# Self-attention of a fused decoder layer: key tile 1 gets its penalties by a multiplication on GpSimd, not by their logs on TensorE

## What is computed

```python
penalties = res * scope                            # (b, 512, 512), from a gate per position
log_pen = jnp.log(jnp.maximum(penalties, 1e-32))
scores = jnp.einsum('bhqd,bhkd->bhqk', q, k) / np.sqrt(16)
scores = scores + log_pen[:, None, :, :]           # the same for all 16 heads
probs = jax.nn.softmax(scores, axis=-1)
ctx = jnp.einsum('bhqk,bhkd->bhqd', probs, v)
```

## Time and profile before

| | us |
|---|---|
| median of 3 runs | 879.59 |
| lowest and highest | 878.59, 881.4 |
| the profiled execution, its own time | 875.29 |
| its span, first to last instruction | 873.5 |

### The profile page before, as it was taken

How to read it: one execution, slowest core, us unless ns; L and a number is a source line. 1 busy time by engine, 2 the same in 40 slices (tenths; PEclk the granted TensorE clock), 3 DMA queues, 4 the chain that set the end, 5 groups by cost and what they waited for, 6 DMA issues and landing times.

```text
span 873.5 us, 12882 instructions
## 1 busy us (share of the span) xinstructions
PE 707.1 (81%) x4374; PEld 279.8 (32%) x4374; DVE 618.0 (71%) x1576; ACT 482.7 (55%) x800; POOL 328.1 (38%) x417
## 2 busy tenths in 40 slices
PE   6077779998788799998898899996798699965653
PEld 3042223343222243443232433532223134332221
DVE  3978674675698756668967556589876577627996
ACT  3213465555354858744458578444467576954634
POOL 6104656645466404445663034555414011000314
PEclk9588899999999989999999899998989899996965
DMA  3532142120322213211222132223112320000002
GB/s 102 147 113 92 40 94 75 57 64 20 91 60 63 86 31 111 78 40 51 65 67 84 29 89 78 60 75 102 39 39 59 88 63 16 6 1 1 1 1 96
DMA packets 34896, 54.00 MB, mean 62 GB/s; under 512 B 4368, under 2 KB 25872, under 8 KB 34832
## 3 DMA queue, kind: packets, MB, share of 16 engines
q1 hardware_dynamic: 32912, 51.61, 20.7%
q10 hardware_dynamic: 1920, 1.57, 1.1%
HBM read 36.91 MB, written 14.68 MB: 59 GB/s over the span
## 4 chain that ended last, share of the span: by engine, by line
PE 44%; DVE 26%; POOL 11%; ACT 9%; issue 7%; DMA 2%; SPq 1%; ACTq 0%; POOLq 0%; DVEq 0%
PE ps L1447 10%; PE ps L1402 9%; DVE unused L931 7%; PE ps L1422 6%; POOL probs L652 6%; PE ps L1389 6%; PE ps L1305 5%; ACT probs L836 3%; PE ps L1382 2%; POOL rest L678 2%; DMA KS<-parts_kc 2%; PE ps L1426 2%; PE ps L1427 1%; DVE pen_a L994 1%; DVE h_all L1218 1%
## 5 line engine op out<-in xcount | busy, mean ns | idle before, releaser
L1402 PE MATMUL ps<-KS,QS 96*128 96x512 bf16 x512 | 202.8, 397 | 79.4 <-DVE mx L931 52.6
L836 ACT ACTIVATE probs<-ps 128x512 f32<-128x512 f32 x256 | 148.8, 596 | 151.5 <-PE ps L1427 96.7
L652 POOL TENSOR_TENSOR probs<-probs,penT 128x512 f32<-128x512 f32 x128 | 166.9, 1322 | 167.9 <-ACT probs L836 167.5
L931 DVE CUSTOM_DVE_ANT_0 unused<-ps,lp 128x512 bf16<-128x512 f32 x256 | 171.1, 686 | 81.9 <-PE ps L1402 77.8
L1422 PE MATMUL ps<-QS,KS 108*128 108x512 bf16 x512 | 198.2, 390 | 11.5 <-ACT probs L836 11.3
L836 ACT ACTIVATE probs<-ps,mask_col 128x512 f32<-128x512 f32 x256 | 166.4, 688 | 59.0 <-PE ps L1422 57.4
L931 DVE CUSTOM_DVE_ANT_0 unused<-ps,mask_rest 128x512 bf16<-128x512 f32 x192 | 128.2, 685 | 48.7 <-PE ps L1402 47.8
L1402 PEld LDWEIGHTS ps<-KS,QS 96*128 96x128 bf16 x512 | 50.5, 99 | 225.5 <-DVE mx L931 125.7
L1447 PE MATMUL ps<-probs,v_s 128*32 128x256 f32 x1024 | 83.8, 400 | 9.6 <-POOL probs L652 8.8
L1447 PE MATMUL ps<-probs,v_c 128*32 128x256 f32 x1024 | 82.5, 395 | 0.6 <-ACT probs L836 0.6
L678 POOL TENSOR_TENSOR rest<-proj,parts 128x512 f32<-128x512 f32 x32 | 38.3, 1197 | 79.4 <-ACT parts L749 78.8
(11 more groups left out here) (186 smaller groups left out, 969.9 us busy)
## 6 DMA issues: line engine op xcount, KB each, us to landing
parts_qs<-parts SPq DMA_DIRECT2D x8, 384.0 KB, 2.6
parts_ks<-parts SPq DMA_DIRECT2D x8, 384.0 KB, 2.8
QS<-parts_qs SPq DMA_DIRECT2D x16, 192.0 KB
KS<-parts_ks SPq DMA_DIRECT2D x16, 192.0 KB
parts_kc<-parts SPq DMA_DIRECT2D x8, 384.0 KB, 2.5
parts_qc<-parts SPq DMA_DIRECT2D x8, 384.0 KB, 2.8
QS<-parts_qc SPq DMA_DIRECT2D x16, 192.0 KB
KS<-parts_kc SPq DMA_DIRECT2D x16, 192.0 KB
```

Of the source, the lines that this page charges most:

```text
L652: g.tensor_tensor(probs[:, T % NP, :], probs[:, T % NP, :], penT[:, MUL_KT.index(kt), :], ALU.mult)\
L836: s_.activation(probs[:, T % NP, :], ps[:, EXP_BANKS[T % 3], :], ACT.Exp, bias=bias)\
L931: v.tensor_tensor_reduce(out=unused[:, i % 2, :], in0=ps[:, MAX_BANKS[i % 2], :], in1=lp[:, t, :] if kind == "s" else mask_row(b), scale=1 ...
L1402: mm(ps[:, MAX_BANKS[i % 2], :], QS[0:SK, slot, j, t * P:(t + 1) * P], KS[0:SK, slot, j, :], start=True, stop=True).then_inc(max_scores, 1)
```

## The change

One constant. `MUL_KT` lists the key tiles whose penalties are multiplied in on GpSimd; `exp_tile`, `context`, `multiply`, `lpB` and the sizes of `penT`, `lpT_hi` and `lpT_lo` all go by it.

```diff
-MUL_KT = (0, 2)
+MUL_KT = (0, 1, 2)
```

## The result

The changed kernel took **897.19 us** (median of five runs, 895.97 to 905.91) beside 879.70 us for the kernel before in the same sitting: 1.0223 times as long, interval 1.0169 to 1.0277. The prediction said 892.9 us, in a range of 881 to 908, and slower. Sign and size are right. Of the three terms that make up the sum, the first came out within its bounds and the third in its total. The second, the largest, was mis-sized by a factor of two: the slower VectorE operations that it counts came, but it left out GpSimd's queue in those groups and the time at TensorE's half clock.

The account below looks back on a forecast made before the run. TensorE was fullest (81% busy), but self groups were taken as paced by PE, DVE or POOL's queue. Terms -1.8 + 7 + 5.6 + 2.5 = +13.3 us on 879.6 gave 892.9 us, range 881 to 908.

Parts of the forecast that it names:

- first term: Seven self groups (s(b,g): batch b, head group g) that PE paces: POOL's queue eats part of TensorE's saving, -1.8 us.
- walk of s(2,1): POOL's queue followed forward in batch 2, head group 1: key tile 2's context product slightly earlier, net -0.7 us, not -1.73.
- second term: Seven self groups that DVE paces: PE's saving becomes waiting, DVE operations slow beside POOL; +7 us, bounds 0 and +14.
- third term: Groups where a projection's split shares POOL's queue: s(1,1) +5.6 us, bounds +3 and +7; s(2,3) +2.5, bounds 0 and +4.
- its own walk to 224.0: POOL's queue followed in s(1,1): the projection's second low part ends at 224.0 instead of 218.44, +5.6 us.
- GpSimd keeps up: Rival: POOL has room, so nine self groups gain 1.73 us each; 864 us, faster. Chance 0.09.
- The waits are absorbed: Rival: new waits for POOL shorten later row-maximum waits and contention is hidden; 881 us, no change. Chance 0.14.
- The waits let the clock fall: Rival: new PE waits bring four to six falls of TensorE's clock, 10 us more; 903 us. Chance 0.17.
- 64 instructions on each line: Sign: the logs' matmul lines L1426 and L1427 stand 64 times each, where they had 128.
- waits for POOL near 20 us: Sign: context products (L1447) waiting for POOL rise from 8.8 us to some 20 to 30 us.
- L990's median above 0.9 us: Sign: the DVE penalty operation on L990, 0.884 us in the median, rises above 0.9 us.
- the longer wait in s(1,1): Sign: PE waits for `KS<-parts_kc` in s(1,1) longer than 3.5 us.

Follow-up runs that it names:

- second profile: Another profiled execution of the changed kernel, unedited, taken with the experiments: 896.73 us, span 894.8 us.
- the order mended: Changed kernel, but in s(1,1) the four added multiplications stand behind the second low part of the projection's split: 892.48 us, ratio 1.0146.
- the repeat: The changed kernel, unedited, timed again in another sitting beside the kernel before: 900.49 us, ratio 1.0220.
- the opposite move: Against the kernel before, only key tile 0 is multiplied on GpSimd; tiles 1, 2 and 3 get their logs on TensorE: 871.56 us, ratio 0.9903.

## Why the prediction was right, point by point

**The first term was right within its bounds.** The walk of s(2,1) had the context product of key tile 2 at 407.8 instead of 408.55, 0.75 us earlier. In the second profile, in which s(2,1) ran at the full clock, PE has it here:

```profile
419.00 0.64 PE L1447 MATMUL ps<-probs,v_s 128*32 128x256 f32 x8 [1.92 <-POOL probs L652]
```

That group began at 398.83, so it is 20.17 us into the group, 20.93 before: 0.76 us. Behind it stand, on POOL, two rstd instructions and the last pair of multiplications, in the order of the walk:

```profile
415.00 0.23 POOL L634 TENSOR_SCALAR rstd<-mv 128x4 f32<-128x4 f32 x1
415.31 1.04 POOL L635 TENSOR_TENSOR rstd<-rstd,minus_half 128x4 f32<-128x4 f32 x1
416.31 2.53 POOL L652 TENSOR_TENSOR probs<-probs,penT 128x512 f32<-128x512 f32 x2
```

The sum of the seven groups was -0.2 and +1.0 us and not -1.8. The half clock came into some of them: s(3,0) took 21.1 us at the full clock in one profile, and 22.7 us with 3.4 us of half clock in the other, the same instructions. That is not so everywhere: s(0,3) took 21.55 us with 3.4 us of it and 21.43 us with none.

**The second term failed in size, by what it left out.** It held TensorE's saving in these seven groups at zero and charged +7 us for slower VectorE operations. The penalty operations slowed down as priced. But the groups lost 15.1 and 13.8 us, and the five of them that hold penalty operations lose as much without these. Two things were left out. POOL, whose twelve multiplications and five short instructions I walked in the groups that PE paces only, can set the pace in these as well (ten in a row at 1.41 us against a slot of 1.33 us in s(2,2)); PE's waits for POOL in the seven groups rose from 2.8 us to 9.5 and 6.8. And half-clock time in them rose from 23.6 us to 63.7 and 58.4. No run tells how the missing 7 or 8 us divide between the two. Windows of s(2,2) in after and in the second profile:

```profile
429.10:452.00 22.90, 18.99 (x113) 5.29 (x112) 21.52 (x48) 10.60 (x18) 18.30 (x17) 0.83 0.22 57
```
```profile
421.40:445.60 24.20, 19.98 (x113) 5.37 (x112) 23.36 (x51) 10.51 (x18) 18.51 (x17) 0.79 0.22 58
```

In the earlier trace rows it has nine PE records more and 17.91 us of PE at clock 1.00; now fewer matmuls, 19 to 20 us of PE, and 0.83 and 0.79. In s(1,2) of after the order of time on PE shows the step itself:

```profile
254.43 0.64 PE L1447 MATMUL ps<-probs,v_s 128*32 128x256 f32 x8 [1.71 <-POOL probs L652]
...
256.12 0.61 PE L1402 MATMUL ps<-KS,QS 96*128 96x512 bf16 x1
256.52 0.63 PE L1422 MATMUL ps<-QS,KS 108*128 108x512 bf16 x1
...
260.14 1.08 PE L1447 MATMUL ps<-probs,v_s 128*32 128x256 f32 x8 [1.28 <-POOL probs L652]
```

A wait of 1.71 us; from 256.12 on the matmuls take 0.61 us and stand 0.40 to 0.43 us apart instead of 0.22, the lower of the two levels; and another wait of 1.28 us follows. TensorE: Matmul & The Clock Gate of the Trainium skill (Part 1) says that activity releases a clock that is throttled otherwise. The trace agrees as to the direction: less activity in the self groups (PE busy for 342.9 of 421.7 us, before 344.3 of 398.0) and 94.7 us of half clock instead of 33.9. It doesn't show that each wait brings a fall, since s(3,1) has one of 1.9 us and, in the second profile, no fall.

**The third term was right in its total and in part in its mechanism.** The low part of s(1,1) ended 5.4 us later in its group (5.6 worked), and with the order mended the kernel gains 6.5 us, give or take 3.6. But the group lost 5.9 us in one profile and 2.6 in the other, below the bound of +3, and a part of either is the half clock (13.7 us instead of 3.4). s(2,3) lost 2.8 and 3.7 us (2.5 worked); no run tests its cause. The two terms' total of 8.1 us stands against 8.7 and 6.3 measured. The prediction counts two and three new multiplications ahead of the two low parts of s(1,1); the order shows one and four, and its own walk to 224.0 used those. I had said that PE's wait for `KS<-parts_kc` would be longer than 3.51 us. It is 3.54 in after and 1.38 in the second profile:

```profile
239.90 0.61 PE L1402 MATMUL ps<-KS,QS 96*128 96x512 bf16 x1 [3.54 <-DMA KS<-parts_kc]
```
```profile
238.31 0.39 PE L1402 MATMUL ps<-KS,QS 96*128 96x512 bf16 x1 [1.38 <-DMA KS<-parts_kc]
```

The transfer is 5.4 us late, and the wait for it isn't, since PE itself came late: POOL held up its context products, and matmuls ahead of this wait ran at the half clock. A wait's length says how late one is against the other, not how late either is.

**The rivals.** *GpSimd keeps up* fell: even with the multiplications left out, the kernel gains 5 us and not 15.6. *The waits are absorbed* fell: the kernel is slower, and PE waits for row maxima no less (52.6 us before, 55.6 and 59.0 after). *The waits let the clock fall* had 0.17 and a price of 10 us on top of the sum. The fall came, with 28 us of longer matmuls against 27.6 us removed. Its price in time isn't shown; the whole shortfall of the sum, 4.3 us and 7.6 us in the repeat, is under those 10 us. The range held because it left room for this: with the second term at its bound of +14, the sum is 20.3 us. The prediction's lower bound of about +1 takes the first term at -1.8; with its stated -5 it is -2.

**Signs.** Right: 64 instructions on each line; waits for POOL near 20 us (19.8); s(2,1) shorter by under 1 us at the full clock; s(2,2) not shorter. Wrong: L990's median above 0.9 us (0.77); the longer wait in s(1,1).

**Open.** No run sets the clock and leaves the rest alone. How the 20 us divide between the waits, the clock and the slower VectorE operations is not shown; the account and the spread between runs point at the clock, while s(2,2) at 24.1 us and full clock shows that a group can lose 3 us without it. Nor is it settled why the same program falls in s(2,1) in one execution and in s(3,0) in another, which makes after's runs differ by 10 us.

## What to carry to other kernels

Before moving work from the fullest engine to an idle one, walk the idle engine's queue against the slot time in *every* kind of stage, not only where the full engine sets the pace: a queue of twelve 1.3 us operations against slots of 1.3 us has no reserve, and half of the added width cost 5 us where the whole cost 24. Then split the span into busy and idle time of the bounding engine: if busy time doesn't fall by the work removed, look at the granted clock. And try the opposite move; here it was the faster one, since TensorE had 166 us of waiting to put work into.

## What was not expected of the hardware

- Matmuls of TensorE that were removed did not come back as time: without them and with nothing in their place, the mean clock went from 0.923 to 0.905 in the profiles, the other matmuls took 13.0 us longer, and the kernel gained 5 us of 27.6.
- Over two profiles of one program a half-clock stretch of 3.4 us went with 1.6 us in one self group (s(3,0), 21.1 and 22.7 us, the same instructions) and with 0.1 us in another (s(0,3), 21.43 and 21.55 us).
- VectorE's seven penalty operations, 112 in all, took 74.8, 88.6 and 94.4 us beside 64, 128 and 192 multiplications on POOL, while the 512 row maxima stayed at 351 us in all three.
- The multiplication on POOL, 1.26 us at its shortest, took 1.41 us over ten in a row in s(2,2), where VectorE is busy for 21.52 of 22.90 us.
